# A count matrix built on the chip: two edge columns of each chunk as straight code, a loop over pairs for the rest

## The reference

```python
dst = jnp.minimum((12500 * jax.random.uniform(key3, (200000,)) ** 2.0).astype(jnp.int32), 99999)
_o = jnp.argsort(dst, stable=True)
...
agg = jax.ops.segment_sum(msg, dst, num_segments=N_NODES)
```

## Time and profile before

| | |
|---|---|
| median of 3 runs | 12794.58 us |
| the profiled execution, its own time | 12813.53 us |
| its span in the trace | 12811.7 us |
| the build, first mark to last copy | 3157 to 5797 us of the span |
| TensorE busy over the span | 7656.7 us (60%) |
| VectorE busy over the span | 5118.7 us (40%) |
| ScalarE busy over the span | 1761.8 us (14%) |

### The profile page before, as it was taken

How to read it: one execution, slowest core, us unless ns; L and a number is a source line. 1 busy time by engine, 2 the same in 40 slices (tenths; PEclk the granted TensorE clock), 3 DMA queues, 4 the chain that set the end, 5 groups by cost and what they waited for, 6 DMA issues and landing times.

```text
span 12811.7 us, 273411 instructions
## 1 busy us (share of the span) xinstructions
PE 7656.7 (60%) x61727; PEld 5494.5 (43%) x61728; DVE 5118.7 (40%) x13474; ACT 1761.8 (14%) x3566; POOL 5615.3 (44%) x5555
## 2 busy tenths in 40 slices
PE   5666666663665555556788444444566655455666
PEld 4555555552112222224455333444555544444566
DVE  4444545546544444443433222333322233322333
ACT  2333333331012222330000000000000000000000
POOL 4666555452000000005530577777654376554554
PEclk7777777776555555557889655566677766666777
DMA  2222222221001111115555322222455566655666
GB/s 59 66 63 63 64 62 61 61 59 36 20 40 54 66 70 70 70 80 169 150 169 176 75 51 56 56 58 58 121 189 173 198 206 232 217 183 199 203 216 202
DMA packets 977744, 1416.34 MB, mean 111 GB/s; under 512 B 540705, under 2 KB 649761, under 8 KB 970914
## 3 DMA queue, kind: packets, MB, share of 16 engines
q1 hardware_dynamic: 689858, 1130.79, 26.0%
q0 software_dynamic: 184832, 224.29, 9.0%
q10 hardware_dynamic: 102752, 58.62, 1.6%
HBM read 1197.73 MB, written 215.36 MB: 110 GB/s over the span
## 4 chain that ended last, share of the span: by engine, by line
PE 31%; issue 23%; DVE 14%; DVEq 14%; POOL 9%; DMA 6%; ACT 1%; SPq 1%; POOLq 0%; ACTq 0%
PE ps_turn L921 13%; POOL ARENA L620 9%; PE ps_turn L884 7%; PE ps_out L776 4%; DMA ARENA<-table_gat,idx 2%; DMA ARENA<-counts 2%; DVE onehots L1700 2%; DVEq L1714 2%; PE ps_pair L776 1%; DMA idx<-src_r 1%; DVEq L392 1%; PE ps_turn L692 1%; PE ps_pair L949 1%; DVE ARENA L1635 1%; DVEq L1630 1%
## 5 line engine op out<-in xcount | busy, mean ns | idle before, releaser
L620 POOL DMA_INDIRECT ARENA<-table_sage,idx x1920 | 1901.7, 990 | 1729.5 <-DVE idx L1695 1192.8
L921 PE MATMUL ps_turn<-ARENA 128*128 128x96 bf16 (+2 forms) x24010 | 2274.4, 262 | 543.0 <-DVE DSUM L1746 215.9
L921 PEld LDWEIGHTS ps_turn<-ARENA 128*128 128x128 bf16 x24010 | 1864.0, 106 | 948.7 <-issue 647.7
L884 PE MATMUL ps_turn<-ARENA 128*128 x3736 | 1515.8, 508 | 1219.5 <-issue 584.4
L620 POOL DMA_INDIRECT ARENA<-table_gat,idx x1568 | 1671.9, 1066 | 1188.1 <-issue 1131.0
L620 POOL DMA_INDIRECT ARENA<-table_gine,idx x1568 | 1541.2, 983 | 964.1 <-issue 950.1
L620 POOL DMA_INDIRECT ARENA<-table_dev,idx x480 | 481.8, 1004 | 2660.0 <-DVE idx L1695 2522.3
L1635 DVE TENSOR_SCALAR ARENA<-ARENA 128x784 f16 x1868 | 902.6, 483 | 1415.9 <-PE ps_turn L884 963.9
L949 PE MATMUL ps_pair<-ARENA,onehots 128*128 128x32 bf16 (+2 forms) x10140 | 699.7, 227 | 997.4 <-DVE ARENA L1707 868.6
L776 PE MATMUL ps_out<-ARENA,onehots 128*128 128x256 f32 (+1 forms) x3136 | 950.0, 472 | 517.7 <-DMA ARENA<-table_gine,idx 368.9
L884 PEld LDWEIGHTS ps_turn<-ARENA 128*128 x3736 | 389.1, 104 | 1959.0 <-issue 1863.2
(11 more groups left out here) (298 smaller groups left out, 6850.4 us busy)
## 6 DMA issues: line engine op xcount, KB each, us to landing
ARENA<-counts SPq DMA_DIRECT2D x1470, 448.0 KB
counts<-ARENA SPq DMA_DIRECT2D x49, 3136.0 KB, 9.0
ARENA<-counts SPq DMA_DIRECT2D x490, 224.0 KB
ARENA<-dst_b SPq DMA_DIRECT2D x393, 256.0 KB
ARENA<-edge_attr SPq DMA_DIRECT2D x390, 128.0 KB, 2.5
ARENA<-table_sage,idx POOLq DMA_INDIRECT x1920
ARENA<-table_gat,idx POOLq DMA_INDIRECT x1568
ARENA<-table_gine,idx POOLq DMA_INDIRECT x1568
```

The costliest lines, as they stand in the source:

```text
L620: pool.indirect_dma_start(ps["buf"][:, s, c, 0:ps["row"]], None, ps["table"][:, :], bass.IndirectOffsetOnAxis(idx[:, s, c:c + 1], 0)).then ...
L884: last = pe.matmul(ps_turn[:, at:at + WIDE_ROW // 2], ring[:, 0:P], ring[:, P + q * (WIDE_ROW // 2):P + (q + 1) * (WIDE_ROW // 2)], start= ...
L921: last = pe.matmul(ps_dense[half][:, 0:n], RING[:, b, :], XP[:, b, :], start=(b == PIECE_AT[pieces[0]]), stop=(j == pieces[-1] and b == PI ...
```

## The change

Every chunk now has two marks as straight code, whether it has two columns with edges or only one. These two have buffers of their own in `MARKS`, chosen by the chunk's parity when the program is written, so no register holds their address. VectorE waits once for a chunk (for `chunk_done` of two chunks ago) in place of once for a mark. Columns after the second are taken in pairs: a loop with `pairs` rounds, skipped by a branch where `pairs` is 0, makes two marks and their four matmuls per round, in a ring of two pairs (`more_ready`, `more_free`). `pairs` is (columns - 1) shifted right by one, worked out on VectorE by two more small operations. A column past the last one with edges, or past the end of the list, yields a mark that counts nothing for the chunk; `KEY` and `AKEY` get two more columns for this, filled by two memsets. The last of the two straight marks closes the chunk's sums, so the matmuls with zeros are gone. `chunk_done` starts at 2.

```diff
-        MARKS = arena(4 * 512, dt=BF16)
+        MARKS = arena(8 * 512, dt=BF16)
...
                     for c in range(4):
-                        lo, hi = pe.snap(bounds[2 * c], min_val=0, max_val=COLS - 1), pe.snap(bounds[2 * c + 1], min_val=1, max_val=COLS)
+                        pairs = pe.snap(bounds[2 * c + 1], min_val=0, max_val=COLS // 2)
+                        at = (c % 2) * 2048
                         pe.wait_ge(chunk_read, i * 4 + (c + 1))
                         settle(pe)
-                        mark(c, True)
-                        with pe.If(lo + 1 < hi):
-                            with pe.Fori(lo + 1, hi) as j:
-                                mark(c, False)
-                        for q in range(2):
-                            at = (c % 2) * 1024 + q * 512
-                            last = pe.matmul(ps_turn[:, at:at + CHUNK], ZERO[:, :], ZERO[:, 0:CHUNK], start=False, stop=True)
-                        last.then_inc(chunk_done, 1)
+                        pe.wait_ge(marks_ready, i * 16 + (4 * c + 2))
+                        settle(pe)
+                        count(c, MARKS[:, at:at + 1024], True, False)
+                        with pe.If(pairs > 0):
+                            with pe.Fori(0, pairs) as e:
+                                pe.reg_add(more, more, 4)
+                                pe.wait_ge(more_ready, pe.snap(more, min_val=1, max_val=2 * CHUNKS * COLS))
+                                settle(pe)
+                                ring = MARKS[:, bass.ds(4096 + pe.snap(half, min_val=0, max_val=2048), 2048)]
+                                count(c, ring[:, 0:1024], False, False)
+                                count(c, ring[:, 1024:2048], False, False).then_inc(more_free, 1)
+                                pe.reg_alu(half, half, 2048, ALU.bitwise_xor)
+                        pe.wait_ge(marks_ready, i * 16 + (4 * c + 4))
+                        settle(pe)
+                        count(c, MARKS[:, at + 1024:at + 2048], False, True).then_inc(chunk_done, 1)
...
+                step(ve.memset(KEY_pad[:, COLS:COLS + 2], -1.0))
+                step(ve.memset(AKEY_pad[:, COLS:COLS + 2], 0.0))
...
+                            at = (c % 2) * 2048
+                            ve.wait_ge(chunk_done, i * 4 + (c + 1))
+                            settle(ve)
+                            for x in range(2):
+                                mark(MARKS[:, at + x * 1024:at + (x + 1) * 1024], i * 4 + c, lo + x, marks_ready)
+                            with ve.If(pairs > 0):
+                                with ve.Fori(0, pairs) as e:
+                                    ve.reg_add(more, more, 1)
+                                    ve.wait_ge(more_free, ve.snap(more, min_val=1, max_val=CHUNKS * COLS))
+                                    settle(ve)
+                                    ring = MARKS[:, bass.ds(4096 + ve.snap(half, min_val=0, max_val=2048), 2048)]
+                                    for x in range(2):
+                                        j = nc.s_assert_within(lo + e * 2 + (2 + x), 0, COLS, skip_runtime_bounds_check_because="2 * pairs <= columns of the chunk - 1")
+                                        mark(ring[:, x * 1024:(x + 1) * 1024], i * 4 + c, j, more_ready)
+                                    ve.reg_alu(half, half, 2048, ALU.bitwise_xor)
```

More of the change, by code:

```diff
@@ L144, in build @@
         ends_in, ends_red, ranges_in, ranges_stored, ranges_loaded = sem("ends_in"), sem("ends_red"), sem("ranges_in"), sem("ranges_stored"), sem("ranges_loaded")
-        marks_ready, marks_free, chunk_done, chunk_read = sem("marks_ready"), sem("marks_free"), sem("chunk_done"), sem("chunk_read")
+        marks_ready, chunk_done, chunk_read = sem("marks_ready"), sem("chunk_done"), sem("chunk_read")
+        more_ready, more_free = sem("more_ready"), sem("more_free")
         counts_stored, stage_free, most_in, most_red = sem("counts_stored"), sem("stage_free"), sem("most_in"), sem("most_red")
@@ L223, in build @@
         STAGE = arena(TILES * P, dt=BF16)
-        MARKS = arena(4 * 512, dt=BF16)
+        MARKS = arena(8 * 512, dt=BF16)
         IOTA16 = arena(WIDE_ROW // 2, dt=F16)
         COL16 = arena(P // 2, dt=F16)
-        KEY, AKEY = arena(COLS), arena(COLS)
+        KEY_pad, AKEY_pad = arena(COLS + 2), arena(COLS + 2)
+        KEY, AKEY = KEY_pad[:, 0:COLS], AKEY_pad[:, 0:COLS]
         BASES = arena(CHUNKS)
@@ L868, in build_tensor, with count @@
             def build_tensor():
-                marks, seen = pe.alloc_register("pe_marks"), pe.alloc_register("pe_seen")
+                half, more = pe.alloc_register("pe_half"), pe.alloc_register("pe_more")
                 bounds = [pe.alloc_register(f"pe_bound{q}") for q in range(8)]
-                pe.reg_mov(marks, 0)
-                pe.reg_mov(seen, 0)
+                pe.reg_mov(half, 0)
+                pe.reg_mov(more, 0)
                 pe.wait_ge(ranges_loaded, 16)
[L876 to L881, removed]
+                def count(c, marks, opens, closes):
                     for q in range(2):
                         at = (c % 2) * 1024 + q * 512
[L884 to L888, removed]
+                        last = pe.matmul(ps_turn[:, at:at + WIDE_ROW // 2], marks[:, 0:P], marks[:, P + q * (WIDE_ROW // 2):P + (q + 1) * (WIDE_ROW // 2)],
+                                         start=opens, stop=closes)
+                    return last
                 with pe.Fori(0, CHUNKS // 4) as i:
@@ L1069, in build_scalar @@
                     for c in range(PER_TILE):
-                        act.wait_ge(chunk_done, t * PER_TILE + (c + 1))
+                        act.wait_ge(chunk_done, t * PER_TILE + (c + 3))
                         settle(act)
@@ L1573, in build_vector @@
                 ve.sem_inc(arena_open, 1)
-                ve.sem_inc(marks_free, 4)
+                ve.sem_inc(chunk_done, 2)
+                ve.sem_inc(more_free, 2)
                 ve.sem_inc(chunk_read, 2)
@@ L1614, in build_vector, with mark @@
                 step(ve.scalar_tensor_tensor(range_ends[:, :, 1], range_ends[:, :, 0], 1.0, range_ends[:, :, 1], ALU.add, ALU.max))
+                step(ve.scalar_tensor_tensor(range_ends[:, :, 1], range_ends[:, :, 1], -1.0, range_ends[:, :, 0], ALU.add, ALU.subtract))
                 step(ve.tensor_copy(range_ends_i, range_ends))
+                step(ve.tensor_scalar(range_ends_i[:, :, 1], range_ends_i[:, :, 1], 1, None, ALU.arith_shift_right))
                 ve.sem_inc(ranges_in, 1)
                 ve.wait_ge(ranges_loaded, 16)
-                marks, seen = ve.alloc_register("ve_marks"), ve.alloc_register("ve_seen")
+                half, more = ve.alloc_register("ve_half"), ve.alloc_register("ve_more")
                 bounds = [ve.alloc_register(f"ve_bound{q}") for q in range(8)]
-                ve.reg_mov(marks, 0)
-                ve.reg_mov(seen, 0)
+                ve.reg_mov(half, 0)
+                ve.reg_mov(more, 0)
+                def mark(marks, q, j, ready):
+                    ve.tensor_scalar(marks[:, P:P + WIDE_ROW], IOTA16, BASES[:, bass.ds(q, 1)], KEY_pad[:, bass.ds(j, 1)],
+                                     ALU.add, ALU.is_equal).then_inc(ready, 1)
+                    ve.tensor_scalar(marks[:, 0:P], COL16, AKEY_pad[:, bass.ds(j, 1)], None, ALU.is_equal).then_inc(ready, 1)
                 def mark_tiles(first, upto):
@@ L1628, in mark_tiles @@
                         for c in range(4):
[L1629 to L1639, removed]
+                            lo, pairs = ve.snap(bounds[2 * c], min_val=0, max_val=COLS - 1), ve.snap(bounds[2 * c + 1], min_val=0, max_val=COLS // 2)
@@ L1645, in build_vector @@
                 mark_tiles(2, KT)
-                ve.wait_ge(chunk_done, CHUNKS)
+                ve.wait_ge(chunk_done, CHUNKS + 2)
                 ve.wait_ge(stage_free, KT + 2)
```

## The result

The changed kernel takes 11767.51 us (median of 4 runs, 11752.12 to 11778.97) against 12792.9 us for the kernel before (median of 4): a ratio of 0.920, 95% interval 0.918 to 0.921, or 1025 us less. The forecast was 11,930, and its range 11,800 to 12,130 does not hold the result: the sign and the place were right, the saving was put at 867 us and is 1025.

The account below looks back on a forecast made before the run. Sequencers, TensorE's above all, were taken to bound the build. 784 x 1.70 + 267 x 1.60 + 13 = 1773 us against 2640 saves 867; 12813.5 - 867 - 19 = 11,928, said as 11,930, range 11,800 to 12,130.

Parts of the forecast that it names:

- The bound before: Build, 2640 us: bound by sequencers working out registers, TensorE's above all; "issue" 33.9% of the chain of waits.
- 0.12 us per instruction, 0.20 for a taken branch: TensorE's and VectorE's sequencers in the build: each register, wait or branch instruction 0.12 us, a taken branch 0.20 more.
- Counts: Marks in the build after the change: 784 x 2 + 267 x 2 = 2102, against 1868; 1568 matmuls with zeros gone.
- 4 x 0.327 = 1.31 us: Straight part on TensorE: a chunk's four matmuls at 1.2 GHz, 1.31 us per chunk in place of 2.53.
- the trip through ScalarE: Matmuls, copy and waits back to the next matmul: 2.99 us for two chunks, 1.50 each, no longer covered.
- The clock as a rival: TensorE in the build rises to 2.4 GHz: 1.58 us per chunk, 1.50 per pair, time 11,807; chance 0.14.
- the two cases: Build at the risen clock, time 11,807, and the forecast with the clock kept at 1.2 GHz, time 11,930.
- VectorE's part, 1.30 us at most: Straight part on VectorE: two marks, each wide 0.40 plus narrow 0.25 us, 1.30 at most, below TensorE's 1.31.
- The hole: Outer loop with its load of eight bounds, every fourth chunk: 1.17 us stays, partly hidden by stock, 0.20 per chunk.
- its upper bound: Outer loop's waits on TensorE and VectorE, slow loads included, both added in full: 0.29 + 0.31 = 0.6 us per chunk.
- A pair at 1.60: Loop over columns after the second: 1.60 us per round of two marks, 267 rounds, 427 us; bounds 1.31 and 2.75.
- Nothing outside the build: Rest of the kernel: untouched; a change there of more than 30 us would make the whole sum wrong.

Follow-up runs that it names:

- The best version: Changed kernel with marks and sums four chunks deep and eight chunks per load of bounds: build 1381 us, 14,911.58 us, ratio 0.9245 to the kernel before.
- the four-deep ones: Changed kernel with stocks four chunks deep in place of two: build 1556 us (marks), 1592 (sums), 1482 (both), against 1607.

## Why the prediction was wrong

- *The bound before.* Right. Sequencers held the build: putting TensorE's registers back cost 767 us, VectorE's 589. "TensorE's above all" is only partly so: VectorE's alone would have held it at 2196.
- *0.12 us per instruction, 0.20 for a taken branch.* Right: 1.00 us per chunk on TensorE's sequencer against 1.04 reckoned; 2.53 and 2.21 per chunk with the registers back against 2.5 and 2.25.
- *Counts.* Right: 2102 marks, 4204 matmuls.
- *"4 x 0.327 = 1.31 us": the step that failed.* I carried the clock of the slow kernel over to the fast one. With the change the grant rose from 0.50 to 0.92. A matmul then starts every 0.165 us, a chunk's four take 0.66 and not 1.31, and the trip through ScalarE, which holds them as its first part, takes 2.46 us for two chunks and not 2.99. With the matmul time put back by the doubled matmuls, the build is 1748 us; so about 141 of the 166 us by which the build was forecast too long are the clock.
- *The clock as a rival.* It was named, priced at 11,807 and given 0.14; the run came out 40 us below even that. Its argument against ("once matmuls are fast, TensorE is busy only half the time, so the grant would not stay") did not hold: the build has a grant of 0.92 with TensorE busy 66% (1060.76 of 1608). By the depth-cycling rule of the Trainium skill ("TensorE: Matmul & The Clock Gate") I had placed the result between the two cases, and it lies below both. The trace shows some of that swing, 0.88 to 0.97 in windows of 200 to 400 us from 3200 us on, but the grant stays mostly at the upper level. The rule of the Trainium skill in the section on why this matters for your kernels ("TensorE: Matmul & The Clock Gate"), to keep TensorE busy without pause, isn't borne out as a condition either: TensorE pauses 0.44 and 1.20 us between groups of eight matmuls in the rows above, and in the kernel before it paused no longer, 0.35 to 0.54 us outside the load, at a grant of 0.50.
- *VectorE's part, 1.30 us at most.* A bound, and too high: the narrow operation lets the next one start after 0.16 us (4602.73 to 4602.89), not 0.25, so two marks are 1.12 us.
- *The hole.* 0.20 per chunk assumed. The best version and the four-deep ones show that such a term exists (1.52 per chunk falls to 1.38 with deeper stocks) and that it comes through the stocks, as argued. Sizes: 0.14 from the stocks, 0.12 more from half the loads. By the chunk times above a load costs (1.00 + 2.20 - 2.46) / 4 = 0.18 per chunk over the trip through ScalarE, and the slow one in every tile (3.41 - 2.20) / 16 = 0.08 more, which the prediction had only in its upper bound.
- *A pair at 1.60.* 1.54; 1.63 with doubled matmuls.
- *Nothing outside the build.* Right within 1 us of 10,170.

## What to carry to other kernels

When an engine is bound by its sequencer, count register, wait and branch instructions and price them from one unhindered round; that number carried over in both directions here. When a change packs TensorE's work closer, don't keep the clock that the loose version was granted: reckon the new term at both levels, give the faster one real weight, and test it by issuing matmuls twice. When several engines wait for one busy engine, shorten that engine's work before believing it is the bound; here a deeper stock on both sides of TensorE was worth 125 us and half the width of VectorE's operation 23. And look whether the shortened work is held by that engine's sequencer, as it was here.

## What the runs showed of the hardware that I had not expected

- TensorE's busy share of a stretch does not tell its clock: 59% at a grant of 0.50 (before), 65% at 0.57 (TensorE's registers back), 65% at 0.92 (before, matmuls twice). At the lower level each record is longer, so the share hides how little is done.
- 3736 further matmuls in the kernel before cost 5 us in all, and the granted clock over the build went from 0.50 to 0.92.
- The load of bounds from on-chip memory into registers takes 592 to 606 ns for eight and 1108 ns for sixteen, at times 1800 ns for eight. Before, that was so on VectorE alone (TensorE once); after, about 40 of 196 on either engine are slow. The traces show when: while a tile's counts are being stored. After SyncE issues that store (L521) its packets move from 0.8 to 8.5 us (medians of 48 stores of the changed kernel). In the changed kernel all 83 slow loads begin 3.3 to 7.7 us after an issue, and no load that begins in that stretch is normal; the 37 slow ones of the kernel before begin 4.1 to 7.7 us after. With eight chunks a load none happens to begin before 8.1 us, and none is slow. Storing at another moment was not tried, so that the store is the cause is not shown by experiment.
- The same build length, 1607 us, came with a rest of 10,170 us in one job and 13,470 to 13,530 us in others; the time of the kernel before moved alike (12,793 and 12,832 us, then 16,117 and 16,126). What lengthens the rest was not tried.
